# A graph and expert block on one core: the cut of 125-row transfers, 120 and 5 rows in place of 112 and 13

## What is computed

```python
xn = _layernorm(x, axis=-1)
x = x + _L0_gnn_ref(xn, src, dst, ...) + _L0_mix_ref(xn[None], ...)[0]
x = x + _L0_ffn_ref(_layernorm(x, axis=-1)[None], ...)[0]
```

```python
fs = (x @ Ws + bs).reshape(-1, H, D)
fd = (x @ Wd + bd).reshape(-1, H, D)
e = jax.nn.leaky_relu(fs[src] + fd[dst], 0.2)
logits = jnp.einsum('ehd,hd->eh', e, attn)
m = jax.ops.segment_max(logits, dst, num_segments=N)
ex = jnp.exp(logits - m[dst])
denom = jax.ops.segment_sum(ex, dst, num_segments=N)
alpha = ex / denom[dst]
out = jax.ops.segment_sum(alpha[:, :, None] * fs[src], dst, num_segments=N)
return jax.nn.elu(out)
```

## Time and profile before

| what | us |
|---|---|
| median of 3 runs | 1382.32 |
| lowest and highest run | 1380.54, 1392.81 |
| the profiled execution, its own time | 1391.27 |
| its span, first to last instruction | 1389.5 |
| busy: PE, DVE, POOL, ACT | 1056.4, 918.9, 605.3, 564.0 |

### The profile page before, as it was taken

The page is one execution under the profiler, slowest core; times in us unless marked ns, Lnnn a source line. Parts: engine busy times, 40 slices in busy tenths (PEclk is TensorE's granted clock), DMA queues, the critical chain, the costliest instruction groups (busy, mean ns, idle before and its releaser), DMA issues.

```text
span 1389.5 us, 16074 instructions
## 1 busy us (share of the span) xinstructions
PE 1056.4 (76%) x5539; PEld 871.2 (63%) x5539; DVE 918.9 (66%) x1650; ACT 564.0 (41%) x736; POOL 605.3 (44%) x581
## 2 busy tenths in 40 slices
PE   5975655555543488798999999917987998999981
PEld 5963433333322488797778777815755997888871
DVE  6648777677774698644444544474467665999993
ACT  3304333333331599310243444411054324777770
POOL 1027777777775000003777777786300000333330
PEclk9988587658895689899699999956987899999995
DMA  9955776666666852237777777858313026999986
GB/s 336 357 192 166 205 206 187 183 184 192 202 201 166 200 116 69 74 100 251 218 233 209 229 225 206 265 169 241 93 71 120 5 102 271 397 404 405 399 334 189
DMA packets 85034, 290.86 MB, mean 209 GB/s; under 512 B 15970, under 2 KB 37768, under 8 KB 84341
## 3 DMA queue, kind: packets, MB, share of 16 engines
q0 software_dynamic: 34656, 145.11, 34.7%
q1 hardware_dynamic: 46822, 130.71, 27.7%
q10 hardware_dynamic: 3488, 14.16, 2.6%
HBM read 258.31 MB, written 31.62 MB: 209 GB/s over the span
## 4 chain that ended last, share of the span: by engine, by line
PE 35%; POOL 32%; issue 12%; DMA 8%; DVE 8%; ACT 3%; SPq 1%; DVEq 0%; POOLq 0%; ACTq 0%
POOL dense_logits L586 12%; POOL ring_s L575 11%; PE ps L1472 10%; PE ps L1473 10%; PE ps L1474 10%; POOL ring_d L581 9%; DMA ring_d<-table_dst,dst_i 4%; PE ps L1569 2%; PE ps L1553 1%; ACT de L728 1%; DMA y_in<-y_rows 1%; DMA dl_b<-dense_logits 1%; DMA dl_a<-dense_logits 1%; PE ps L1503 1%; PE ps L1726 1%
## 5 line engine op out<-in xcount | busy, mean ns | idle before, releaser
L575 POOL DMA_INDIRECT ring_s<-table_src,src_i x168 | 179.3, 1067 | 319.9 <-DVE fd_stage L947 256.0
L1532 PE MATMUL ps<-hot_s,hot_d 128*125 128x512 f16 (+1 forms) x840 | 186.2, 388 | 157.5 <-DVE hot_s L1028 157.5
L1532 PEld LDWEIGHTS ps<-hot_s,hot_d 128*125 128x125 f16 x840 | 116.7, 180 | 227.2 <-DVE hot_s L1028 167.9
L586 POOL DMA_INDIRECT dense_logits<-logits,cell_i x168 | 191.9, 1143 | 56.7 <-issue 50.2
L581 POOL DMA_INDIRECT ring_d<-table_dst,dst_i x168 | 164.1, 977 | 76.4 <-issue 50.6
L1065 DVE SCALAR_TENSOR_TENSOR ring_d<-ring_s,ps 128x768 f32<-128x768 f32 x84 | 80.1, 953 | 146.6 <-DMA ring_d<-table_dst,dst_i 146.1
L1021 DVE TENSOR_TENSOR ring_s<-ring_s,ring_d 128x776 f32<-128x776 f32 (+1 forms) x168 | 160.8, 957 | 16.8 <-DMA ring_d<-table_dst,dst_i 16.8
L702 ACT ACTIVATE hot_d<-iota_h,dst_bias 128x626 f16<-128x626 f16 x84 | 68.6, 816 | 223.2 <-PE ps L1532 223.2
L1037 DVE TENSOR_REDUCE head_sum<-ring_s 128x8 f32<-128x768 f32 x84 | 80.0, 953 | 81.7 <-DMA ring_d<-table_dst,dst_i 81.1
L1472 PE MATMUL ps<-wp,at 128*125 128x384 f32 x300 | 106.8, 356 | 11.4 <-issue 4.4
L614 POOL COPY gather_i<-lst 128x1 int32 (+1 forms) x16 | 7.4, 464 | 237.9 <-DVE lst L1392 142.6
(11 more groups left out here) (253 smaller groups left out, 2368.2 us busy)
## 6 DMA issues: line engine op xcount, KB each, us to landing
eraw<-in_moe_w_dram SPq DMA_DIRECT2D x50, 768.0 KB, 6.9
raw<-in_moe_w_dram SPq DMA_DIRECT2D x44, 768.0 KB, 7.1
dense_logits<-neg ACTq DMA_DIRECT2D x1, 12288.0 KB, 40.7
mix_w<-in_qkv_wT_dram SPq DMA_DIRECT2D x18, 384.0 KB, 5.8
dl_a<-dense_logits SPq DMA_DIRECT2D x2, 2187.5 KB
dl_b<-dense_logits SPq DMA_DIRECT2D x2, 2187.5 KB
y_in<-y_rows SPq DMA_DIRECT2D x5, 672.0 KB
ring_s<-table_src,src_i POOLq DMA_INDIRECT x168, 4.2
```

Source lines behind the costliest of these rows:

```text
L575: pool.indirect_dma_start(out=ring_s[:, j, 0:WL[l]], out_offset=None, in_=table_src[l], in_offset=bass.IndirectOffsetOnAxis(ap=src_i[:, t: ...
L586: pool.indirect_dma_start(out=dense_logits[l], out_offset=bass.IndirectOffsetOnAxis(ap=cell_i[:, t:t + 1], axis=0), in_=logits[:, t, 0:HL[ ...
L1532: last = pe.matmul(ps[0:P, b, o:o + s1 - s0], hot_d[:, j, c * P:(c + 1) * P], hot_s[:, j, s0:s1], start=start and (n <= 5 or n == 9), stop ...
```

## The change

One constant. The large piece of every 125-row transfer has 120 rows in place of 112, and the small one 5 in place of 13:

```diff
 W = 6
 CELLS = 128 * 3072
 NEG_W = 1024
-PARTS = ((0, 112), (112, 125))
+PARTS = ((0, 120), (120, 125))
 HEADS1 = 8
 DX = D + HEADS1
 MH = 12
```

## The result

The kernel with 120 and 5 rows took 1396.21 us, the median of 18 runs (1383.82 to 1410.65). The kernel before, in 18 runs too, took 1383.45 (1376.52 to 1397.28). The ratio is 1.008 with a 95% interval of 1.0052 to 1.0108: 0.8% slower, about 11 us, and the interval leaves out 1. Ratios here leave out executions over 1.5% above the fastest of their kernel, which is why they differ a little from the ratio of the two medians. The slowdown is within the 1% named in the prediction and the time inside its range of 1375 to 1398, but it is nearly twice the +6 that it forecast.

A forecast was written before the change was run, and what follows sets the result against it. The prediction took PE and POOL to hold two thirds of the chain, DMA 8%, exposed 125-row transfers being limited by shape. Terms 1.37 + 1.37 + 0.67 + 1.84 + 0.8 = +6.05 us, on 1382.3, gave 1388.4; own range 1384 to 1393, wider range 1375 to 1398.

The forecast's parts named there:

- the prediction's picture: All 125-row tiles: rows go in equal shares to as many of 16 engines as divide them; busiest carries 9, not 8.
- the 1.0 of the forecast: Second load of x: lands 1.0 us later, costed at nothing because PE needs the freed bank only later, cover 4.5 us.
- So each exposed tile costs one row more on its busiest engine: Exposed loads and stores of 125-row tiles: each lengthens by one row's time, 1.37 us for a row of 20,000 bytes.
- dl_a +1.37 and dl_b +1.37: First two layer-0 logits loads: each 1.37 us longer, one row of 20,000 bytes more, with DVE waiting on them.
- y_in +1.84: y_in loads at the end: five tiles back to back, each one row of 0.37 us longer, +1.84 us together.
- layer-1 logits +0.67: Layer-1 logits loads: five tiles queued back to back, each one row of 0.134 us longer, +0.67 us together.
- a table_dst store +0.2: Last table_dst store of each layer: 0.2 us longer, estimated from load rates; part of +0.8 for four small transfers.
- the eights: Eights collide, the second rival: with 8 rows an engine, engines may meet at the same part of SBUF; chance 0.25.
- The second rival: Eights collide in SBUF: load stretches at half the 128-row rate, +12 us (1394), up to +19 (1401); chance 0.25.
- Its harder form: Second rival, each tile ending its 5 rows before the next begins: +19 us with small tiles, 1401; within the 0.25.
- The first rival: Bytes bound, not the deepest engine: load rates stay, 15 engines carry what 16 did; no change, 1382; chance 0.22.
- The third: Remainder is the slow part: fewer remainder rows shorten dl_a and dl_b by 2.4 us each; -7.8, 1374.5; chance 0.15.

The follow-up runs named there:

- run 7: Kernel after, with the logits of both layers and y_in cut 112 and 13 again, the rest 120 and 5: 1388.83 us beside 1385.83 before, ratio 1.0017.
- run 3: Kernel before (112 and 13), SP waiting for the large piece of dl_a and every y_in tile before issuing the small one: 1402.63 us, one execution.
- run 8: Kernel before, logits and y_in tiles loaded as one DMA of 128 rows, last y_in tile cut 117 and 8: 1375.26 us beside 1385.83, ratio 0.9916.
- run 2: Kernel after with all pairs cut 117 and 8 in place of 120 and 5: 1381.58 us beside 1382.28 before, ratio 1.0014.
- run 4: Kernel after (120 and 5), SP waiting for the large piece of dl_a and every y_in tile before issuing the small one: 1403.16 us, one execution.
- run 1: Kernel after with all pairs cut 105 and 20 in place of 120 and 5: 1389.6 us beside 1382.28 before, ratio 1.003.

## Why the prediction was right and wrong

The dl_a load in one place (large piece as engines x rows; the busiest engine with the remainder's rows on top). The packet counts bear out the sums of engines; that rows go in blocks, and the remainder on top, is the prediction's picture:

| cut | large piece | busiest engine, rows | dl_a, us |
|---|---|---|---|
| 112 + 13, before | 16 x 7 | 8 | 13.23 (12.81 in run 7) |
| 105 + 20 | 15 x 7 | 9 | 12.34 |
| 117 + 8 | 13 x 9 | 10 | 11.32 |
| 120 + 5, after | 15 x 8 | 9 | 16.39 |
| 5 + 120, remainder in front | 15 x 8 | 9 | 16.07 |
| 104 + 21 | 13 x 8 | 11 | 17.20 |
| 128 alone, with issue | 16 x 8, order unknown | 8 | 9.47 |

*The frame held.* The growth that the chain shows lies where the prediction placed it, in dl_a, dl_b, the layer-1 logits, y_in and the small stores, and it adds up to the ratio. Where the prediction put nothing, none is seen: no wait for dl_c or the later loads; PE's products paced DVE after the second load of x as before (16.1 us of waiting at L1111, 17.6 in the earlier trace rows). The wait for that load grew from 10.3 to 11.4, as the 1.0 of the forecast wants, but runs 3 and 8, which load it with 112 and 13, have 11.9 and 11.2, so this is not shown. SP's issues before dl_a and dl_b stayed short, 0.32 to 0.34 us. The engine counts held, by the packets.

*The step that failed* is "So each exposed tile costs one row more on its busiest engine", with its prices dl_a +1.37 and dl_b +1.37. They measured +3.16 and +3.71. The price took 1.37 us for a row from the dl_b stretch and held it fixed while the shape changed. Run 2 refutes the law itself (10 rows, the shortest cut load), and run 4 its size (the large piece alone +3.32). In its place stands this: a row has no fixed price; it depends on the cut, and in these runs it was high whenever the engines had blocks of 8. With blocks of 8 the 120 rows need 14.25 us; less the 2.3 for start and landing that the prediction used, that is 1.49 a row. With blocks of 7 it is (10.93 - 2.3) / 7 = 1.23. The 2.3 itself was worked out from the 1.37 that failed; by the estimate from two row lengths (runs 3 and 4) the prices are 1.57 and 1.34.

*The other terms* came out too small as well, by less: y_in +1.84 forecast, +2.42 behind the last issue (1.0 a tile when the pieces stand apart); layer-1 logits +0.67 against +1.09; a table_dst store +0.2 against +0.45 and +0.83. That the term for y_in came within a third is no support for its reason, and that the total landed inside the range is in part luck: 1375 to 1398 was wide enough for several of the theories. The prediction said the dl_b stretch would show 208 GB/s, and that 202 or less with dl_a at 15 to 16 us would speak for the eights; it showed 184, and dl_a 16.4.

*The second rival* was the case that came: +12 at its lower end, against about 11 measured and 11.7 by the pieces. Its split was off, though. It placed +1.7 on each dl load and +4.6 on y_in, where +3.2, +3.7 and +2.4 came. Its harder form, in which a tile ends its 5 rows before the next begins, had +3.4 for each dl load, close to what came, and +7.0 for y_in, far off. On y_in a tile's small piece may still be moving while the next tile's large one begins; whether this is the reason was not tried by itself. What I had held against this rival was that 128-row transfers have eights and are the fastest. It was a poor argument, for nothing showed that those rows go to the engines in blocks; run 8 shows them fast in this very load.

For the mechanism the runs show this much for dl_a: cuts with blocks of 8 are slow on 15 engines (16.39) and on 13 (17.20), and with the large piece beginning at row 0 or 5; cuts with blocks of 7 and 9 are not; a remainder of 5 rows costs as much as one of 13 (4.44, 4.33). The rows an engine writes, and in what order, no trace shows. One rival was not tried: every run moves the rows in DRAM together with the partitions, so the collision could also lie on the DRAM side. Against it speaks that the extra time of 120 rows goes with the bytes, 3.32 us for dl_a and 1.0 for y_in (0.31 of the bytes), although blocks of 8 start 160,000 bytes apart in the one source and 49,152 in the other.

The Trainium skill, SBUF — State Buffer, section "Door 1: The DMA port swizzle", has a rule that would give this, if each engine writes a block of neighbouring rows in step with the others: four neighbouring partitions share one of 16 ports, so blocks that start 8 apart meet on 8 of them, up to two engines to a port, at some 27 GB/s a port. An estimate from that page is 20,000 bytes at half of 27, which is 1.48 us a row and 11.9 for eight rows, to which the 2.3 of start and landing are added: 14.2, where run 4 measured 14.25. That it fits this closely is partly luck: with the 1.7 fixed that two row lengths give, it would be 13.6, and the row measured 1.57. By the same rule 4 of the 13 rows of the old remainder share a port, and 4 of the 5 of the new one, so both should take alike; the runs have 4.33 and 4.44. The Trainium skill, DMA: Bandwidth & Descriptors, section "The descriptor swizzle", gives each engine of a 128-row transfer a port of its own. The 9.47 us of run 8 are in keeping with it; no trace shows the ports.

*The first rival*, bytes, falls with the ratio of 1.008 and with the loads of run 2. *The third*, a slow remainder, falls with the result itself, since it had dl_a shorter, and with runs 3 and 4.

Open are the long y_in, dl_b and logits of run 1 (15.05, 14.04, 6.75), why the second table_dst store from SBUF grows with every other cut (2.96 us before, 3.29 with 105 and 20, 3.34 with 117 and 8, 3.79 with 120 and 5, 4.49 with 104 and 21), on which side of the transfer the eights meet, and whether 117 and 8 alone make the kernel faster, as its loads are.

## What to carry to other kernels

When a tile has fewer than 128 rows, count not only how many DMA engines a transfer gets but how many rows each of them would carry: with 7 or 9 rows an engine dl_a was short here, with 8 it was long (12.3 and 11.3 us against 16.4), and 13 engines at 9 rows beat 15 at 8. Measure all the loads, though, since 105 and 20 helped dl_a alone, and no two-piece cut was shown to make the whole kernel faster. Better still was one load of 128 rows, where the source has rows to read behind the tile and the buffer has 128 partitions: it was the fastest (9.5 us), and such loads made this kernel 0.8% faster. A rate read from a trace belongs to the shape it was read from.

## What the runs showed that I had not expected

- A cut whose large piece has only 13 engines had the fastest dl_a of the cuts (the other such cut, 104 and 21, had the slowest): DMA share 0.61 and 221 GB/s in the dl_a stretch of 117 and 8, share 0.73 and 153 GB/s with 120 and 5. A high busy share of the DMA engines was no sign of more bytes moved.
- A DMA of 5 rows of 20,000 bytes took 4.44 us, one of 13 rows 4.33.
- Stores of the tables from SBUF suffer most with eights too: 2.36 and 2.96 us with 112 and 13, 2.50 and 3.34 with 117 and 8, 2.81 and 3.79 with 120 and 5, 3.60 and 4.49 with 104 and 21.
- The count of packets on the page fits the number of engines that a DMA uses: 51 pairs, 9 packets fewer a pair, as 29 engines became 20.
